# Attention rows of three slots in four chains, in place of four slots in three chains

## The chip, the cores and the metric

The kernel runs on one core of one Trainium2 chip. The metric is the device time of one execution in microseconds (us), lower is better. An engine is named as the profile names it: PE (TensorE), DVE (VectorE), ACT (ScalarE), POOL (GpSimd), SP (SyncE, which only issues DMAs here).

## The reference

A graph network on 6250 nodes and 100000 edges (`src`, `dst`, sorted by `dst`), 256 features. First three layers of max-pooling over incoming edges with two layer norms, then one layer of sparse attention with 8 heads whose rows are the sources and whose columns are the destinations of the edges:

```python
h = jnp.maximum(_layernorm(x), 0.0)
x = x + L0(h, src, dst)            # pool-max over edges, matmul, relu, layer norm: three times
h = jnp.maximum(_layernorm(x), 0.0)
q = (h @ Wq + bq).reshape(n, 32, 8) * 32 ** -0.5
k, v = (h @ Wk + bk).reshape(n, 32, 8), (h @ Wv + bv).reshape(n, 32, 8)
s = einsum('edh,edh->eh', q[src], k[dst])
m = segment_max(s, src); e = exp(s - m[src]); z = segment_sum(e, src)
out = segment_sum((e / z[src])[:, None, :] * v[dst], src)
x = x + out.reshape(n, -1) @ Wo + bo
```

## The kernel before

**Stages.** A projection; then three times a pass over the edges (`max_pass`, 87 batches of nine gathers, each gather 128 rows of 1 KB) and a pass over the nodes (`combine`, the last one `combine_project`, 49 tiles); then the attention pass, the carry over the ends of its chains (`carry_attention`), and a last pass over the nodes (`finish`). Each stage is a block with its own instruction list for every engine; `staged` writes those lists out so that stages of several batches interleave.

**Rows and slots.** For the attention the edges are sorted by source on the chip (during passes 1 and 2) and laid out in rows. A row belongs to one source node and holds up to `SLOT` = 4 of its edges; a node with more edges has several rows, one after the other; empty slots are masked by `empty`. Each of the 128 partitions holds `RP` = 234 rows, cut into `R` = 3 chains of `NBA` = 78 rows. In batch n every partition works on row n of each of its chains, so a batch has R x SLOT = 12 slots of 128 edges. A row hands its running maximum, sums and weighted values (`state`, 272 numbers) on to the next row of its chain if both are of the same node (`row_reset`, `row_fresh`). Where a node goes over the end of a chain, `carry_attention` joins the parts by scans over all 128 x R = 384 chain ends.

**A batch of the attention pass.** POOL issues one indirect gather for each slot (L1871): 128 rows of 2 KB, key and value, into `kv`, six batches of buffers deep. DVE multiplies the keys by the row's query (L1903, `multiply`, which waits for all twelve gathers of its batch), weighs the values of the batch before (L1909, `weigh`), sums the products by head (L1913), scales what the chain brings in (L1928, `hold`), masks (L1934), copies the next batch's new queries over the old ones (L1892, `renew`, `copy_predicated` with the mask `row_fresh`), finds the maximum (L1940) and adds up the state (L1945, L1956, L1950, L1960). ACT takes one exponential (L1985). PE adds the weighed values over the slots by identity matmuls (L1977). SP stores the state (L2000) and loads the queries of a later batch (L1995).

**What prepares it.** In pass 1 `Degrees` counts edges by node and finds the rows of each node (`own_rows`, L1019 to L1023: add SLOT - 1, shift right by 2) as small DVE instructions between the folds of the max. `RowNodes` (L1338 to L1352, beside the first `combine`) finds the node of each row: comparisons on DVE and two matmuls a tile into `total`, 234 columns. `Marks` makes the resets of the rows at the start of pass 3. `Spread`, beside pass 3, moves the 936 edges of a partition to their slots: 16 steps of `aim`, then 40 of `move`, two steps a batch. `Clear` zeroes the query table `qtab` in pass 2, one 384 KB store a batch. The query table is filled by scatters in `combine_project`.

**Memory.** The eight PSUM banks are three tensors, `trio`, `wide` and `tail`. The attention pass keeps the queries in `wide`, the sums over slots in `tail` and `trio`.

Of the kernel before, what the change touches and what calls it, by code (L numbers as in the profile page):

```python
# [19 lines left out]
F32, BF16, I32, I16 = mybir.dt.float32, mybir.dt.bfloat16, mybir.dt.int32, mybir.dt.int16  # L20
ALU, ACT, AX = mybir.AluOpType, mybir.ActivationFunctionType, mybir.AxisListType

P = 128
D = 256
# [6 lines left out]
ACC = D + HEADS  # L31
KV = 2 * D
STATE = ACC + HEADS
SLOT = 4
R = 3
UN = 7
J = 9
C = 3
STEPS = J // C
UB = 3  # L40
W = 1024
COLS = W.bit_length() - 1
LEVELS = COLS + P.bit_length() - 1
# [59 lines left out]
def gnn_kernel(nc, x, src, dst, wp1, bp1, wm1, bm1, wm2, bm2, wm3, bm3, g2, b2, g3, b3,  # L103
# [14 lines left out]
    RP = NBA * R  # L118
    SL = RP * SLOT
    NOROW = P * RP  # L120
    assert 0 < TAIL < P and 0 < LASTE < CH and PAD >= N and NBA % UB == 0


# [20 lines left out]
    with ExitStack() as top:  # L144
# [33 lines left out]
        nmr = sb(top, "nmr", [P, NT])  # L178
        rows_upto = sb(top, "rows_upto", [P, NT])
        rows_own = sb(top, "rows_own", [P, NT])  # L180
        trio = top.enter_context(nc.psum_tensor("trio", [P, 3 * 512], F32))
        wide = top.enter_context(nc.psum_tensor("wide", [P, 3 * 512], F32))
        tail = top.enter_context(nc.psum_tensor("tail", [P, 2 * 512], F32))
        bank = [t[:, n * 512:(n + 1) * 512] for t in (trio, wide) for n in range(3)] + [tail[:, n * 512:(n + 1) * 512] for n in range(2)]
        bank = bank[0:3] + [bank[6]] + bank[3:6] + [bank[7]]

# [702 lines left out]
        class Degrees:  # L889
# [116 lines left out]
            def own_rows(self, v):  # L1006
                v.wait_ge(s_pe.sem, s_pe.base + 1)
                for n, to in enumerate((self.by_dst, self.by_src)):
                    for half in range(2):
                        rows_of = slice(half * self.LOW, (half + 1) * self.LOW)  # L1010
                        cols = slice(n * self.HIGH + half, (n + 1) * self.HIGH, 2)
                        if half == n:
                            chain.inc(v.tensor_copy(to[rows_of, :], self.f_sums[rows_of, cols]))
                            yield
                        else:
                            chain.inc(v.tensor_scalar(to[rows_of, :], self.sums[rows_of, cols], -1.0, None, ALU.mult))
                            yield
                v.wait_ge(chain.sem, chain.base)
                chain.link(v.tensor_scalar(self.f_ti, self.by_src, SLOT - 1.0, None, ALU.add))  # L1019
                yield  # L1020
                chain.link(v.tensor_scalar(self.f_ti, self.f_ti, SLOT.bit_length() - 1, None, ALU.logical_shift_right))
                yield
                chain.link(v.tensor_copy(rows_own[:, :], self.f_ti))  # L1023
                v.sem_inc(s_dve.sem, 1)
                yield

# [130 lines left out]
        class Spread:  # L1157
# [53 lines left out]
            def vector(self, v):  # L1211
                def find(i, b):
                    if i * UB + b == self.FIND:
                        v.wait_ge(self.looked, 16 * R)
                        v.wait_ge(chain.sem, self.need)
                        v.tensor_tensor(self.at[:, :], self.first[:, 0, 0:1], self.own[:, :], ALU.add).then_inc(self.found, 1)
                        chain.inc(v.tensor_copy(chain_ix[:, :], self.first[:, :, 1]))
                        chain.link(v.scalar_tensor_tensor(out=row_fresh, in0=self.node, scalar=float(N), in1=self.fresh, op0=ALU.is_lt, op1=ALU.mult))

                def slot(at):  # L1220
                    def stage(i, b):
                        q = 2 * (i * UB + b - self.BEGIN) + at
                        if q < 0:
                            return
                        if q < 16:
                            self.aim(v, q)
                        elif q < 16 + 4 * COLS:
                            self.move(v, (q - 16) % 4, COLS - 1 - (q - 16) // 4)
                        elif q < 18 + 4 * COLS:
                            self.put(v, q - 16 - 4 * COLS)  # L1230
                    return stage
                return {1: [(0, find)], 2: [(0, slot(0))], 5: [(0, slot(1))]}

            def aim(self, v, q):
                a, b, ti, window = (x[:, :] for x in (self.a, self.b, self.ti, self.window))
                c = self.c
                one = ones[:, 0:1].to_broadcast([P, SL])
                if q == 0:
                    v.wait_ge(self.taken, 16)
                v.wait_ge(chain.sem, self.need)  # L1240
                if q == 0:
                    ins = v.tensor_scalar(ti, window, NODES.bit_length() - 1, None, ALU.logical_shift_right)
                elif q == 1:
                    ins = v.tensor_copy(a, ti)
                elif q == 2:
                    ins = v.tensor_tensor(b[:, 1:SL], a[:, 1:SL], a[:, 0:SL - 1], ALU.not_equal)
                elif q == 3:
                    ins = v.tensor_tensor(b, b, self.iota, ALU.mult)
                elif q == 4:
                    ins = v.tensor_tensor_scan(c, one, b, 0.0, ALU.mult, ALU.max)  # L1250
                elif q == 5:
                    ins = v.tensor_tensor(ti, self.iota, c, ALU.subtract)
                elif q == 6:
                    ins = v.tensor_scalar(ti, ti, SLOT - 1, None, ALU.bitwise_and)
                elif q == 7:
                    ins = v.tensor_copy(a, ti)
                elif q == 8:
                    ins = v.tensor_scalar(b, a, 0.0, None, ALU.is_equal)
                elif q == 9:
                    ins = v.tensor_tensor_scan(c, one, b, 0.0, ALU.mult, ALU.add)  # L1260
                elif q == 10:
                    ins = v.scalar_tensor_tensor(out=c, in0=c, scalar=float(SLOT), in1=a, op0=ALU.mult, op1=ALU.add)
                elif q == 11:
                    ins = v.tensor_scalar(ti, window, NODES - 1, None, ALU.bitwise_and)
                elif q == 12:
                    ins = v.tensor_scalar(a, ti, 1.0, None, ALU.add)
                elif q == 13:
                    ins = v.scalar_tensor_tensor(out=b, in0=c, scalar=-float(SLOT), in1=self.iota, op0=ALU.add, op1=ALU.subtract)
                elif q == 14:
                    ins = v.scalar_tensor_tensor(out=b, in0=b, scalar=float(NODES), in1=a, op0=ALU.mult, op1=ALU.add)  # L1270
                elif q == 15:
                    ins = v.scalar_tensor_tensor(out=self.value, in0=c, scalar=float(SL + SLOT), in1=b, op0=ALU.is_lt, op1=ALU.mult)
                self.need = chain.inc(ins)

# [31 lines left out]
        class RowNodes:  # L1306

            def __init__(self, space):  # L1310
                parts, start = [], 0
                for size in (RP, RP, UN * P, UN * P, UN * RP, 2 * RP):
                    parts.append(space[:, start:start + size])
                    start += size
                self.iota, self.all1, eq, gt, ge, ti = parts
                self.eq, self.gt, self.ge = (x.rearrange("p (u e) -> p u e", u=UN) for x in (eq, gt, ge))
                self.ti = ti.bitcast(I32)
                self.made, self.mm = Count(sem("node_made"), 0), Count(sem("node_mm"), 0)
                self.total = bank[7][:, 0:RP]
                self.const0 = const_base[0]  # L1320
                const_base[0] += 1
# [512 lines left out]
        def attention_pass(st, state, empty):  # L1834
            KB, QB = 6, 4
            kvs = [sb(st, f"kv{b}", [P, SLOT * R, KV]) for b in range(KB)]
            rooms = [weights[:, b * R * D:(b + 1) * R * D] for b in range(QB - 1)] + [pass_lists[:, b * R * D:(b + 1) * R * D] for b in range(2)]
            *qs, begun = (room.rearrange("p (r f) -> p r f", f=D) for room in rooms)
            held = sb(st, "held", [P, R, ACC])
            s = sb(st, "s", [P, SLOT + 1, R, HEADS])  # L1840
            row_max = sb(st, "row_max", [P, R, HEADS])
            w = shifted.rearrange("p (b e r h) -> p b e r h", b=UB, r=R, h=HEADS)
# [171 lines left out]
        def carry_attention(state):  # L2014
# [3 lines left out]
            with ExitStack() as st, block() as blk:  # L2018
# [8 lines left out]
                add = sb(st, "add", [P, R, ACC])  # L2027
                turned = [bank[k][:, 0:ALL] for k in range(4)]
                made, blocked = sb(st, "made", [P, ALL]), sb(st, "blocked", [P, ALL])
                carried = wide.rearrange("p (r x) -> p r x", r=R)  # L2030
                m0 = s_misc.base

                def chains_of(ap):
# [191 lines left out]
        w_q, w_kv = mat(w_q), mat(w_kv)  # L2225
        w_o, v_o, empty, shifted = parts_of(FREED, KC * D, D, SL, UB * (SLOT + 1) * R * HEADS)
        w_o = mat(w_o)
        assert max(KC * D + KC * KV + D + KV, 3 * R * D) <= FREED

        def find_empty(v):  # L2230
            chain.link(v.tensor_scalar(empty[:, :], dst_ix[:, 0:SL], 0.0, NEG, ALU.is_lt, ALU.mult))
# [2 lines left out]
        with scope() as l0:  # L2234
# [23 lines left out]
            with scope() as g:  # L2258
# [5 lines left out]
                    marks = Marks(c, dst_ix, CH, reset, fix_ix, flag, degrees.hot[:, :].bitcast(F32), C)  # L2264
                    max_pass(G, degrees, LayerInput(c, w_m1a, v_m1, True), marks)
                blocked = sb(g, "blocked", [P, P * C])
                combine(G, U, w_m1b, None, None, True, Carry(G, blocked, 1), RowNodes(G[1][:, :, :].rearrange("p k f -> p (k f)").bitcast(BF16)))
                with scope() as c:
                    clear = Clear(c)
                    max_pass(G, Sorting(sort, clear), LayerInput(c, w_m2a, v_m2, False), ahead=clear)  # L2270
# [42 lines left out]
```

## Time and profile before

| | |
|---|---|
| time, median of 3 runs (lowest to highest) | 4856.15 us (4855.05 to 4858.15) |
| the profiled execution: its own time, its span | 4848.88 us, 4847.1 us |
| busy share of the span: POOL, DVE, PE, ACT | 71%, 65%, 35%, 23% |
| attention gathers on POOL (L1871) | 936 times, 987 ns |
| max-pass gathers on POOL (L541) | 2349 times, 949 ns |

The span is that of one execution, from its first to its last instruction. A group of instructions is shown as line, engine, operation, output<-inputs, shapes, count, then busy time in all, mean ns of one, and the engine's idle time before them with what ended most of it. DMA-issuing instructions of SP are not counted as busy; the gathers on POOL are. In a timeline a row is start, duration, engine, line, operation, and in square brackets the engine's idle time before it and what ended it.

### The profile page before, as it was taken

How to read it: one execution, taken by the hardware profiler on the slowest of the kernel's cores; microseconds unless marked ns; L12 is line 12 of the kernel's file. 1: busy time of each engine (PE TensorE's matmuls, PEld its weight loads, DVE VectorE, ACT ScalarE, POOL GpSimd, SP SyncE). 2: the span in 40 equal slices, each digit the busy share in tenths (PEclk: the TensorE clock that was granted, in tenths of full speed). 3: DMA queues.
4: the chain of work that ended last, by engine and by line, in shares of the span. 5: the costliest groups of instructions: out<-in, count | busy, mean ns of one | idle time of the engine just before them, and what ended most of it. 6: DMA issues, size and time to landing. Idle time of an engine off the chain costs nothing. (4 is left out here: it accounts for less than half of the span.)

```text
span 4847.1 us, 27940 instructions
## 1 busy us (share of the span) xinstructions
PE 1710.1 (35%) x5261; PEld 1035.5 (21%) x5261; DVE 3135.9 (65%) x6298; ACT 1096.5 (23%) x2585; POOL 3461.3 (71%) x3612
## 2 busy tenths in 40 slices
PE   5434322106233312025222200019644454445546
PEld 4222211005111100014111100006322222222224
DVE  7888887645444444437455533338488888888886
ACT  5333322223222222224222222225200000000001
POOL 4777777766777777766777777765377777777764
PEclk8555555558555555557555555559867777777778
DMA  5666666656777777756666766655478887887875
GB/s 193 217 209 210 211 210 209 212 181 209 255 257 255 259 248 242 242 189 209 223 212 221 233 212 209 211 185 192 143 239 256 253 254 255 257 255 255 253 227 178
DMA packets 451437, 1083.65 MB, mean 224 GB/s; under 512 B 82637, under 2 KB 178524, under 8 KB 451263
## 3 DMA queue, kind: packets, MB, share of 16 engines
q0 software_dynamic: 203376, 598.29, 42.7%
q1 hardware_dynamic: 247886, 483.58, 26.9%
q14 instruction: 131, 1.07, 0.1%
q8 instruction: 44, 0.72, 0.1%
HBM read 656.78 MB, written 425.20 MB: 223 GB/s over the span
## 5 line engine op out<-in xcount | busy, mean ns | idle before, releaser
L541 POOL DMA_INDIRECT G<-tab,pass_lists x2349 | 2228.3, 949 | 725.0 <-issue 714.8
L561 DVE SCALAR_TENSOR_TENSOR G<-tail,pass_lists,G 128x256 f32<-128x256 f32 x1566 | 699.1, 479 | 1304.5 <-DMA G<-tab,pass_lists 1296.3
L1871 POOL DMA_INDIRECT kv<-kvtab,dst_ix x936 | 923.5, 987 | 285.1 <-issue 285.1
L602 ACT ACTIVATE tail<-G 128x512 f32<-128x512 f32 x783 | 471.0, 602 | 1768.1 <-DVE G L561 1726.3
L678 PE MATMUL tail<-weights,hT 128*128 128x256 f32 x588 | 304.9, 674 | 551.7 <-ACT hT L655 551.7
L1977 PE MATMUL tail<-kv,ident 128*128 128x512 f32 (+1 forms) x624 | 301.7, 653 | 360.9 <-DVE kv L1909 360.9
L1977 PE MATMUL trio<-kv,ident 128*128 128x512 f32 (+1 forms) x624 | 294.4, 640 | 295.4 <-DVE kv L1909 295.4
L604 ACT ACTIVATE wide<-G 128x256 f32<-128x256 f32 x783 | 296.8, 379 | 382.4 <-DVE G L561 371.1
L561 DVE SCALAR_TENSOR_TENSOR G<-wide,pass_lists,G 128x256 f32<-128x256 f32 x783 | 372.5, 476 | 0.8
L1903 DVE TENSOR_TENSOR kv<-kv,wide 128x3072 f32<-128x3072 f32 x78 | 261.7, 3355 | 167.9 <-DMA kv<-kvtab,dst_ix 167.9
L672 PE MATMUL tail<-ident,h 128*128 128x128 f32 x294 | 95.1, 426 | 625.5 <-DVE U L641 582.3
L678 PEld LDWEIGHTS tail<-weights,hT 128*128 128x128 f32 x588 | 172.6, 324 | 634.6 <-ACT hT L655 608.1
L1985 ACT ACTIVATE wide<-weights 128x120 f32<-128x120 f32 x78 | 21.4, 274 | 1205.9 <-DVE weights L1960 1205.9
L1977 PEld LDWEIGHTS tail<-kv,ident 128*128 128x128 f32 x624 | 157.6, 260 | 505.4 <-DVE kv L1909 377.0
L1909 DVE TENSOR_TENSOR kv<-kv,wide 128x3072 f32<-128x3072 f32 x78 | 261.1, 3347 | 0.3 <-ACT wide L1985 0.3
L1913 DVE TENSOR_REDUCE s<-kv 128x96 f32<-128x3072 f32 x78 | 261.0, 3346 | 0.0
L1379 PE MATMUL trio<-ident,G 128*128 128x128 f32 x18 | 4.5, 424 | 697.0 <-PEq L526 697.0
L1977 PEld LDWEIGHTS trio<-kv,ident 128*128 128x128 f32 x624 | 154.4, 255 | 435.4 <-DVE kv L1909 311.1
L1104 PE MATMUL trio<-hot 128*128 128x196 bf16 x783 | 142.2, 369 | 195.7 <-DVE hot L955 195.7
L672 PEld LDWEIGHTS tail<-ident,h 128*128 128x128 f32 x294 | 42.0, 201 | 734.3 <-issue 689.7
L955 DVE TENSOR_TENSOR hot<-wide,key_high 128x2156 bf16<-128x2156 f32 x72 | 170.4, 2367 | 0.0
L1104 PEld LDWEIGHTS trio<-hot 128*128 128x128 bf16 x783 | 114.1, 148 | 218.7 <-DVE hot L955 207.7
(340 smaller groups left out, 3281.4 us busy)
## 6 DMA issues: line engine op xcount, KB each, us to landing
hist<-G SPq DMA_DIRECT2D x783, 384.0 KB, 3.0
G<-tab,pass_lists POOLq DMA_INDIRECT x2349, 3.2
ahist<-state SPq DMA_DIRECT2D x78, 408.0 KB, 3.4
qtab<-zeros SPq DMA_DIRECT2D x78, 384.0 KB, 4.3
weights<-qtab SPq DMA_DIRECT2D x59, 384.0 KB, 5.7
tab<-o SPq DMA_DIRECT2D x147, 128.0 KB
kv<-kvtab,dst_ix POOLq DMA_INDIRECT x936, 3.9
h<-tab SPq DMA_DIRECT2D x98, 128.0 KB, 3.9
```

The source lines that it names most:

```text
L541: g.indirect_dma_start(G[b][:, k, :], None, tab, bass.IndirectOffsetOnAxis(src_ix[:, at:at + 1], 0)).then_inc(s_in[r].sem, 16)
L561: ins = v.scalar_tensor_tensor(out=G[b][:, k, :], in0=state2 if c == 2 else state[:, c, :], scalar=reset[:, at:at + 1], in1=G[b][:, k, :], ...
L602: a.activation(state, of[:, 0:2, :], ACT.Copy).then_inc(c_state.sem, 1)
L604: a.activation(state2, of[:, 2, :], ACT.Copy).then_inc(c_state.sem, 1)
L678: m = pe.matmul(self.product, self.hT[:, k * P:(k + 1) * P], self.w[:, k, :], start=(k == 0), stop=(k == KC - 1))
L955: v.tensor_tensor(to[n % self.RING][:, 0:some, :, :].rearrange("p k l e -> p (k l) e"), self.iota[:, None, 0:width].to_broadcast([P, 2 * s ...
L1104: m = pe.matmul(self.sums, self.low[n % self.RING][:, k, :, :], self.high[n % self.RING][:, k, :, :], start=(n == 0 and k == 0), stop=(n = ...
L1871: g.indirect_dma_start(kvs[n % KB][:, k, :], None, kvtab, bass.IndirectOffsetOnAxis(dst_ix[:, at:at + 1], 0)).then_inc(s_kv[n % KB], 16)
L1903: v.tensor_tensor(keys, keys, query[:, None, :, :].to_broadcast([P, SLOT, R, D]), ALU.mult).then_inc(c_scored, 1)
L1909: v.tensor_tensor(vals, vals, by_slot[:, :, None, :].to_broadcast([P, GATHERS, HD, HEADS]), ALU.mult).then_inc(c_weighed, 1)
L1913: keep("sums", i * UB + b, v.tensor_reduce(scores().rearrange("p e r h -> p (e r) h"), kvs[(i * UB + b) % KB][:, :, 0:D].rearrange("p k (h ...
L1977: m = pe.matmul(sums[n % 2][:, rs, :], ident[:, :], kvs[n % KB][:, e * R + rs.start:e * R + rs.stop, D:KV], start=(e == 0), stop=(e == SLO ...
```

## The change

`SLOT` becomes 3 and `R` becomes 4. With 6250 nodes and 100000 edges that makes 300 rows a partition in four chains of 75, 900 slots, and 75 batches of twelve gathers; states and queries of a batch have four rows in place of three (stores of 544 and loads of 512 KB in place of 408 and 384). Division by 4, a shift or a mask, becomes division by 3: in `own_rows` by the helper `divide` (ten steps), in `aim` by a multiplication by 683 and a shift by 11. Row numbers now go over 256, so `RowNodes` counts in float32, in place of bfloat16. The carry needs four banks for its 128 x 4 chain ends, so PSUM becomes one tensor of which the old ones are parts. Some buffers of the attention pass move.

```diff
-SLOT = 4
-R = 3
+SLOT = 3
+R = 4
...
+SHIFT = 11
+THIRD = -(-(1 << SHIFT) // SLOT)
...
-        trio = top.enter_context(nc.psum_tensor("trio", [P, 3 * 512], F32))
-        wide = top.enter_context(nc.psum_tensor("wide", [P, 3 * 512], F32))
-        tail = top.enter_context(nc.psum_tensor("tail", [P, 2 * 512], F32))
+        psum = top.enter_context(nc.psum_tensor("psum", [P, 8 * 512], F32))
+        trio, wide, tail = psum[:, 0:3 * 512], psum[:, 3 * 512:6 * 512], psum[:, 6 * 512:8 * 512]
...
-                chain.link(v.tensor_scalar(self.f_ti, self.by_src, SLOT - 1.0, None, ALU.add))
+                chain.link(v.tensor_scalar(self.f_has, self.by_src, SLOT - 1.0, None, ALU.add))
                 yield
-                chain.link(v.tensor_scalar(self.f_ti, self.f_ti, SLOT.bit_length() - 1, None, ALU.logical_shift_right))
-                yield
-                chain.link(v.tensor_copy(rows_own[:, :], self.f_ti))
+                yield from divide(v, self.f_has, SLOT, rows_own[:, :], self.f_stepped[0], self.f_ti, self.f_stepped[1])
...
                 elif q == 5:
-                    ins = v.tensor_tensor(ti, self.iota, c, ALU.subtract)
+                    ins = v.tensor_tensor(a, self.iota, c, ALU.subtract)
                 elif q == 6:
-                    ins = v.tensor_scalar(ti, ti, SLOT - 1, None, ALU.bitwise_and)
+                    ins = v.tensor_scalar(ti, a, float(THIRD), None, ALU.mult)
                 elif q == 7:
-                    ins = v.tensor_copy(a, ti)
+                    ins = v.tensor_scalar(ti, ti, SHIFT, None, ALU.logical_shift_right)
                 elif q == 8:
+                    ins = v.tensor_copy(b, ti)
+                elif q == 9:
+                    ins = v.scalar_tensor_tensor(out=a, in0=b, scalar=-float(SLOT), in1=a, op0=ALU.mult, op1=ALU.add)
...
-                for size in (RP, RP, UN * P, UN * P, UN * RP, 2 * RP):
+                for size in (RP, UN * P, UN * P, UN * RP):
                     parts.append(space[:, start:start + size])
                     start += size
-                self.iota, self.all1, eq, gt, ge, ti = parts
+                self.iota = counted
+                self.all1, eq, gt, ge = parts
...
-                self.ti = ti.bitcast(I32)
+                self.ti = counted.bitcast(I32)
...
-            rooms = [weights[:, b * R * D:(b + 1) * R * D] for b in range(QB - 1)] + [pass_lists[:, b * R * D:(b + 1) * R * D] for b in range(2)]
-            *qs, begun = (room.rearrange("p (r f) -> p r f", f=D) for room in rooms)
+            rooms = [weights[:, b * R * D:(b + 1) * R * D] for b in range(QB - 2)] + [pass_lists[:, 0:R * D]]
+            qs = [room.rearrange("p (r f) -> p r f", f=D) for room in rooms] + [sb(st, "q", [P, R, D])]
             held = sb(st, "held", [P, R, ACC])
+            begun = held[:, :, 0:D]
...
-                carried = wide.rearrange("p (r x) -> p r x", r=R)
+                carried = psum[:, 3 * 512:7 * 512].rearrange("p (r x) -> p r x", r=R)
```

Nothing else is rewritten; all loops and tiles over `R`, `SLOT`, `RP`, `SL` and `NBA` take the new sizes.

## Rows read from the trace of the kernel before

**Rows 1.** The page, part 1: busy time, share of the span and instructions of each engine.

```profile
PE 1710.1 (35%) x5261; PEld 1035.5 (21%) x5261; DVE 3135.9 (65%) x6298; ACT 1096.5 (23%) x2585; POOL 3461.3 (71%) x3612
```

**Rows 2.** The page, part 5: the gathers on POOL.

```profile
L541 POOL DMA_INDIRECT G<-tab,pass_lists x2349 | 2228.3, 949 | 725.0 <-issue 714.8
...
L1871 POOL DMA_INDIRECT kv<-kvtab,dst_ix x936 | 923.5, 987 | 285.1 <-issue 285.1
```

**Rows 3.** Busy time by stretch: mid attention pass, carry, first combine.

```profile
3640.00:4540.00 900.00, 445.43 (x926) 233.30 (x927) 786.83 (x754) 15.90 (x58) 688.32 (x696) 0.72 0.81 255
4735.90:4768.80 32.90, 6.93 (x26) 5.39 (x26) 13.31 (x23) 1.08 (x2) 6.04 (x6) 0.60 0.14 43
1077.00:1152.00 75.00, 65.80 (x392) 54.30 (x392) 46.36 (x197) 33.66 (x97) 50.43 (x52) 0.91 0.57 174
```

**Rows 4.** Waits from 3650 to 4800 us: total, times, longest.

```profile
DVE kv L1903 <- DMA kv<-kvtab,dst_ix: 134.4, 69, 2.5
```

**Rows 5.** Timeline: first and last of the 78 multiplies of the attention pass.

```profile
3517.89 3.35 DVE L1903 TENSOR_TENSOR kv<-kv,wide 128x3072 f32<-128x3072 f32 x1 [12.61 <-DMA kv<-kvtab,dst_ix]
...
4711.21 3.35 DVE L1903 TENSOR_TENSOR kv<-kv,wide 128x3072 f32<-128x3072 f32 x1 [1.98 <-DMA kv<-kvtab,dst_ix]
```

**Rows 6.** Timeline of two batches of the attention pass, POOL and DVE, cut.

```profile
4008.11 0.94 POOL L1871 DMA_INDIRECT kv<-kvtab,dst_ix  x1 [0.30 <-issue]
...
4009.36 1.03 POOL L1871 DMA_INDIRECT kv<-kvtab,dst_ix  x1 [0.30 <-issue]
4009.49 0.96 DVE L1892 COPY_PREDICATED wide<-row_node,weights 128x768 f32<-128x768 int32 x1
...
4010.70 0.94 POOL L1871 DMA_INDIRECT kv<-kvtab,dst_ix  x1 [0.30 <-issue]
...
4013.20 3.35 DVE L1903 TENSOR_TENSOR kv<-kv,wide 128x3072 f32<-128x3072 f32 x1 [1.24 <-DMA kv<-kvtab,dst_ix]
...
4023.19 0.95 POOL L1871 DMA_INDIRECT kv<-kvtab,dst_ix  x1 [0.30 <-issue]
...
4024.32 0.96 DVE L1892 COPY_PREDICATED wide<-row_node,weights 128x768 f32<-128x768 int32 x1
4024.44 1.64 POOL L1871 DMA_INDIRECT kv<-kvtab,dst_ix  x1 [0.30 <-issue]
...
4028.66 3.35 DVE L1903 TENSOR_TENSOR kv<-kv,wide 128x3072 f32<-128x3072 f32 x1 [1.90 <-DMA kv<-kvtab,dst_ix]
```

**Rows 7.** Timeline: a copy and the gather begun under it, early and late.

```profile
3559.35 0.96 DVE L1892 COPY_PREDICATED wide<-row_node,pass_lists 128x768 f32<-128x768 int32 x1
3559.44 1.68 POOL L1871 DMA_INDIRECT kv<-kvtab,dst_ix  x1 [0.30 <-issue]
...
4706.78 0.96 DVE L1892 COPY_PREDICATED wide<-row_node,weights 128x768 f32<-128x768 int32 x1
...
4706.89 1.66 POOL L1871 DMA_INDIRECT kv<-kvtab,dst_ix  x1 [0.30 <-issue]
```

**Rows 8.** Groups by shape: three DVE instructions of the attention pass.

```profile
L1903 DVE TENSOR_TENSOR kv<-kv,wide 128x3072 f32<-128x3072 f32 x78 | 261.7, 3355 | 167.9 <-DMA kv<-kvtab,dst_ix 167.9
...
L1928 DVE TENSOR_TENSOR held<-state,wide 128x792 f32<-128x792 f32 x78 | 75.6, 970 | 0.0
L1892 DVE COPY_PREDICATED wide<-row_node,weights 128x768 f32<-128x768 int32 x59 | 56.7, 961 | 0.0
```

**Rows 9.** DMA queues from 3700 to 4600 us: packets, MB, engine share.

```profile
q0 software_dynamic: 55659, 182.41, 66.6%
q1 hardware_dynamic: 16704, 47.05, 14.0%
```

**Rows 10.** Timeline of the first combine, one tile, cut.

```profile
1107.25 0.26 PE L1345 MATMUL tail<-G 128*128 128x234 bf16 x1
...
1107.35 0.26 PE L1346 MATMUL tail<-G 128*128 128x234 bf16 x1
...
1107.45 0.43 DVE L1530 TENSOR_TENSOR G<-wide,U 128x256 f32<-128x256 f32 x1 [0.34 <-PE wide L1602]
```

More of the change, by code:

```diff
@@ L120, in gnn_kernel @@
     NOROW = P * RP
+    assert all((n * THIRD) >> SHIFT == n // SLOT for n in range(SL))
     assert 0 < TAIL < P and 0 < LASTE < CH and PAD >= N and NBA % UB == 0
@@ L1224, in stage @@
                             return
-                        if q < 16:
+                        if q < 18:
                             self.aim(v, q)
-                        elif q < 16 + 4 * COLS:
-                            self.move(v, (q - 16) % 4, COLS - 1 - (q - 16) // 4)
                         elif q < 18 + 4 * COLS:
-                            self.put(v, q - 16 - 4 * COLS)
+                            self.move(v, (q - 18) % 4, COLS - 1 - (q - 18) // 4)
+                        elif q < 20 + 4 * COLS:
+                            self.put(v, q - 18 - 4 * COLS)
                     return stage
@@ L1251, in aim @@
                 elif q == 5:
-                    ins = v.tensor_tensor(ti, self.iota, c, ALU.subtract)
+                    ins = v.tensor_tensor(a, self.iota, c, ALU.subtract)
                 elif q == 6:
-                    ins = v.tensor_scalar(ti, ti, SLOT - 1, None, ALU.bitwise_and)
+                    ins = v.tensor_scalar(ti, a, float(THIRD), None, ALU.mult)
                 elif q == 7:
-                    ins = v.tensor_copy(a, ti)
+                    ins = v.tensor_scalar(ti, ti, SHIFT, None, ALU.logical_shift_right)
                 elif q == 8:
+                    ins = v.tensor_copy(b, ti)
+                elif q == 9:
+                    ins = v.scalar_tensor_tensor(out=a, in0=b, scalar=-float(SLOT), in1=a, op0=ALU.mult, op1=ALU.add)
+                elif q == 10:
                     ins = v.tensor_scalar(b, a, 0.0, None, ALU.is_equal)
-                elif q == 9:
+                elif q == 11:
                     ins = v.tensor_tensor_scan(c, one, b, 0.0, ALU.mult, ALU.add)
-                elif q == 10:
+                elif q == 12:
                     ins = v.scalar_tensor_tensor(out=c, in0=c, scalar=float(SLOT), in1=a, op0=ALU.mult, op1=ALU.add)
-                elif q == 11:
+                elif q == 13:
                     ins = v.tensor_scalar(ti, window, NODES - 1, None, ALU.bitwise_and)
-                elif q == 12:
+                elif q == 14:
                     ins = v.tensor_scalar(a, ti, 1.0, None, ALU.add)
-                elif q == 13:
+                elif q == 15:
                     ins = v.scalar_tensor_tensor(out=b, in0=c, scalar=-float(SLOT), in1=self.iota, op0=ALU.add, op1=ALU.subtract)
-                elif q == 14:
+                elif q == 16:
                     ins = v.scalar_tensor_tensor(out=b, in0=b, scalar=float(NODES), in1=a, op0=ALU.mult, op1=ALU.add)
-                elif q == 15:
+                elif q == 17:
                     ins = v.scalar_tensor_tensor(out=self.value, in0=c, scalar=float(SL + SLOT), in1=b, op0=ALU.is_lt, op1=ALU.mult)
@@ L1306, in gnn_kernel, with __init__ @@
         class RowNodes:
-            def __init__(self, space):
+            def __init__(self, space, counted):
                 parts, start = [], 0
-                for size in (RP, RP, UN * P, UN * P, UN * RP, 2 * RP):
+                for size in (RP, UN * P, UN * P, UN * RP):
                     parts.append(space[:, start:start + size])
                     start += size
-                self.iota, self.all1, eq, gt, ge, ti = parts
+                self.iota = counted
+                self.all1, eq, gt, ge = parts
                 self.eq, self.gt, self.ge = (x.rearrange("p (u e) -> p u e", u=UN) for x in (eq, gt, ge))
-                self.ti = ti.bitcast(I32)
+                self.ti = counted.bitcast(I32)
                 self.made, self.mm = Count(sem("node_made"), 0), Count(sem("node_mm"), 0)
@@ L2227, in gnn_kernel @@
         w_o = mat(w_o)
-        assert max(KC * D + KC * KV + D + KV, 3 * R * D) <= FREED
+        assert max(KC * D + KC * KV + D + KV, 2 * R * D) <= FREED
         def find_empty(v):
@@ L2266, in gnn_kernel @@
                 blocked = sb(g, "blocked", [P, P * C])
-                combine(G, U, w_m1b, None, None, True, Carry(G, blocked, 1), RowNodes(G[1][:, :, :].rearrange("p k f -> p (k f)").bitcast(BF16)))
+                combine(G, U, w_m1b, None, None, True, Carry(G, blocked, 1), RowNodes(G[1][:, :, :].rearrange("p k f -> p (k f)").bitcast(BF16), G[0][:, :, :].rearrange("p k f -> p (k f)")[:, J * D - RP:]))
                 with scope() as c:
```

## Prediction

> **What bounds the kernel now.** I read the page first, then busy time by stretch, then, for the attention pass alone, its waits, its timeline and its DMA queues. Over the whole span no engine is full; GpSimd (POOL) is busiest, at 71% [rows 1]. The instruction groups say why: 2349 gathers of the three max passes at 949 ns and 936 of the attention pass at 987 ns, each with about 0.30 us of "issue" before it, so nothing else is being waited for between them [rows 2]. The change is aimed at the 936. In that pass a batch is 12 gathers, one batch of DVE work, one load and one store. In the middle of the pass DVE is busy 87% and POOL 76% [rows 3], but POOL's share leaves out its 0.30 us a gather. What ends last is told by the wait: DVE's first instruction of a batch waits for its gathered rows, 69 times in that stretch and never over 2.5 us [rows 4]. So the pass runs at POOL's pace, DVE close behind. First to last multiply is 1193.3 us for 77 steps: 15.50 us a batch [rows 5].
>
> Ten gather steps take 12.49 us (4010.70 to 4023.19), 1.249 each, so twelve free ones are 14.99 us; the other 0.5 us is one slow gather a batch. The timeline shows which. The gather at 4024.44 takes 1.64 us in place of 0.95. It starts 0.12 us after COPY_PREDICATED (L1892, the new query rows, on DVE), which ends at 4025.28, and the gather ends 0.80 after that. One batch earlier the gather starts 0.13 us before the copy and takes 1.03 [rows 6]. First and last such pair of the pass again end 0.81 apart; in 74 batches, those caught all end 0.80 to 0.82 after the copy, those begun before it (seven) are nearly free [rows 7]. So a gather begun under the copy waits for its end: stall = length of the copy - start offset - 0.14.
>
> The Trainium skill (SBUF — State Buffer, Who interferes with whom) has the reason: a DVE instruction with two SBUF inputs takes the port that GpSimd reads through, and the later of the two blocks to its end. The copy reads mask and rows from SBUF, so the rule fits the 0.80. By it alone each batch's stall would lengthen with the copy, and the sum would be -12 us (the second rival); by the offsets of the rows it is -58.
>
> **The change, part by part.**
> *Gathers.* 78 batches of 12 become 75 of 12: 936 to 900. Each stays 128 rows of 2 KB. Worth 3 batches, if a batch costs the same.
>
> *DVE per batch.* The big three keep 3072 elements (12 slots either way). What goes by rows grows by a third: L1928 792 to 1056 elements, L1892 and L1950 768 to 1024. L1903's 3355 ns for 3072 elements against L1892's 961 for 768 make 1.04 ns an element [rows 8], so +0.28, +0.27 and +0.27 us; I put 0.03 for the short instructions. DVE now needs 87.4% of 15.50 us a batch, 13.55; it becomes 14.40. That is under the 14.99 of twelve free gathers, so DVE does not become the bound, but its slack falls from 1.95 to about 0.6.
>
> *TensorE.* 8 identity matmuls of 512 or 256 columns become 6 of 512, the same 3072 columns; PE is half idle there [rows 3]. Nothing.
>
> *DMA.* Software queue 66.6% and hardware queue 14.0% of 15.5 us are 10.3 and 2.2 us of engine time a batch [rows 9]. The load and store grow by a third, +0.72 us: 13.2 us, 87% of a 15.1 us batch. It still fits; if it did not, 14.99 is the floor anyway.
>
> *The stall.* This decides. I follow where the first gather after a batch's last one starts, relative to the copy. If the gather is caught, that last gather's rows come late too: the next multiply starts 3.38 us after the copy's end (4025.28 to 4028.66). If it is free, the multiply starts 5.09 us after the last gather's start (4008.11 to 4013.20); other free batches have 4.9 to 5.0. Multiply to copy is 11.12 us. Now, after a caught batch (offset and stall make 0.96 - 0.14 = 0.82 together, whatever the offset), the next offset is 14.99 + 0.82 - 0.96 - 3.38 - 11.12 = +0.35 (less where rows land later, 0.26 on average): caught again. After a free one it is 14.99 + 1.25 - 5.0 - 11.12 = +0.12: caught again as well. So the old batch always falls back under the copy. After the change the copy is 1.23 long and 11.40 after the multiply. After a caught batch: 14.99 + 1.09 - 1.23 - 3.38 - 11.40 = +0.07, or -0.02 with the later landing: a toss-up. After a free one: 14.99 + 1.25 - 5.0 - 11.40 = -0.16: the gather starts before the copy and is free, and so is the next. Free batches keep themselves free; the second gather starts at +1.09, when the copy has 0.14 us left, which costs nothing. With landing times scattering by 0.1 us, a run of free batches seldom ends and a run of caught ones ends soon. I take one batch in ten caught at 1.05 us and 0.05 us for the rest of the copy or later landings: 15.15 us. Lower bound: no stall, 14.99. Upper bound: always caught just behind the copy's start, 14.99 + 1.07 = 16.06.
>
> 74 steps of 15.15 are 1121.1 against 1193.3: **-72.2 us** (-84 to -5).
>
> *Before and behind the pass.* One more begun gather ahead of the first kv gather, 1.25 (L1871's step). The tail behind the last multiply repeats L1928, L1950 for two more batches, +0.8. The carry works on 512 columns in place of 384: in its stretch of 32.9 us DVE is busy 13.3, PE 6.9, ACT 1.1 [rows 3], nearly all in a chain; a third of that is 7.1, less what PE overlaps and fixed parts, 6.3; the four scatters in place of three add 1.3. Its gathers are covered by the scans. Together +7.6 (6 to 9).
>
> *combine, first layer.* The count of L1345/L1346 multiplies 128x234, now 128x300, two a tile. PE runs without gaps there (65.8 of 75 us busy) [rows 3], a 128x234 bf16 matmul starts 0.10 us after the other, a 128x300 one would take 0.028 more, so +0.055 a tile, 49 tiles: +2.7. The comparison (L1338) reads float32 in place of bf16. If it goes at the 1.04 ns an element of rows 8, I estimate +0.25 a tile, and DVE sits idle 0.34 us before each tile's sum [rows 10]: hidden; without that cover it would be 12 us. Bounds +1 to +12.
>
> *The passes.* Pass 3 gets one more before_row gather on POOL, the bound: +1.25. The eight more steps of the row division are small DVE fillers in pass 1, where POOL's gathers at 0.95 + 0.30 us set the pace [rows 2]: hidden, 2 us if not. Two more steps in Spread, but each of some 60 on 900 in place of 936 elements: hidden, and as SBUF-to-SBUF work it may hold up a gather or two, ±1. Marks over 300 columns delay DVE 1 us while POOL fills 27 tiles: hidden. The clearing stores of pass 2 are 512 KB in place of 384, 75 in place of 78; a gather there still costs POOL its 1.25 us, and I expect POOL to stay the bound. 0 to +3. I put 0.5 for all of these.
>
> Sum: -72.2 + 1.25 + 0.8 + 7.6 + 2.7 + 1.25 + 0.5 = **-58 us**. The profiled run took 4848.88 with a span of 4847.1, and becomes 4791; the median of the three timed runs is 7.3 higher, 4856.15, and becomes **4798**.
>
> **Rivals.** A change under 0.2%, 9.7 us, is what this measurement can't tell from none.
> 1. *The stall stays 0.5 us.* Batches cost 15.50: 74 x 15.50 is -46.4, with +14.1 elsewhere -32: 4824. For it: the mean has been steady for 74 batches. Against it: the offsets above, which move by 0.28.
> 2. *The stall grows by the copy's 0.27* (15.77): -26.3 + 14.1 = -12: 4844. Same evidence against it.
> 3. *Locked behind the copy's start, the other side.* Every batch is caught at +0.0 to +0.1, and the larger load and store delay the last rows. From 16.07 us a batch the kernel is slower by over 0.2%: 74 x 16.07 = 1189.2, -4.1 + 14.1 = +10: 4866. For it: the +0.07 above. Against it: below 0.02 the gather slips free, and a later landing pushes it there.
> 4. *The passes don't hide their parts* (combine's DVE becomes its bound, +9; DMA in pass 2, +3): 4810. Adds to any of them.
>
> **Chances and range.** Slipping free 0.50 (4798, its own range 4785 to 4812, from 14.99 and from 15.3 us a batch); rival 1 0.22; rival 2 0.13; rival 3 0.10, half of it at 16.0 and thus within 0.2%; the rest 0.05, spread. Leaving out the lowest and what lies above rival 2, the range is 4785 to 4852. Faster: 0.50 + 0.22 + most of rival 2 and of the rest, 0.83. Same 0.10. Slower 0.07.
>
> **What the profile after would show.** L1871: 900 times, mean near 955 ns in place of 987; if it is 987, rival 1, 1010 rival 2, 1030 or more rival 3. Multiply to multiply 15.1 us; L1892 1.23 us at 11.40 behind the multiply; the first gather 0.1 to 0.3 us ahead of it. Carry near 40 us. I am wrong if L1892 costs something else than by element (the offset turns on 0.1 us), if more DMA work makes the last rows land later by several tenths, or if other two-input instructions on DVE catch the second gather.

## The result, and the profile after

| | before | after |
|---|---|---|
| time, median of 22 runs (lowest to highest) | 4853.6 us (4848.25 to 4858.36) | 4846.31 us (4823.35 to 4852.61) |
| ratio after/before, 95% interval | | 0.9981 (0.9974 to 0.9987) |
| profiled execution: its own time, its span | 4848.88 us, 4847.1 us | 4838.44 us, 4836.5 us |

Faster by 7 us, within the 0.2% that was called no change; the forecast was 58 us. The time lies in the range, the gain does not come near the one forecast. The time after also scatters over 29 us from run to run, the time before over 10.

The page after, part 5: the gathers of the max passes and of the attention pass, and its first multiply (answer to [rows 2, 8]).

```profile
L543 POOL DMA_INDIRECT G<-tab,pass_lists x2349 | 2225.5, 947 | 726.4 <-issue 714.6
...
L1877 POOL DMA_INDIRECT kv<-kvtab,dst_ix x900 | 917.4, 1019 | 274.2 <-issue 270.8
...
L1909 DVE TENSOR_TENSOR kv<-kv,psum 128x3072 f32<-128x3072 f32 x75 | 251.6, 3354 | 134.2 <-DMA kv<-kvtab,dst_ix 134.2
```

36 gathers are gone, but one takes 1019 ns on average in place of 987. Against the 946 of gathers that nothing holds up (experiment 1), 12 x (1019 - 946) is 0.88 us of stall a batch, where 0.5 was. The max passes have not moved.

The timeline after: first and last multiply (answer to [rows 5]).

```profile
3520.95 3.35 DVE L1909 TENSOR_TENSOR kv<-kv,psum 128x3072 f32<-128x3072 f32 x1 [12.38 <-DMA kv<-kvtab,dst_ix]
...
4696.30 3.35 DVE L1909 TENSOR_TENSOR kv<-kv,psum 128x3072 f32<-128x3072 f32 x1 [1.46 <-DMA kv<-kvtab,dst_ix]
```

1175.35 us for 74 steps, 15.88 a batch in place of 15.50: the pass gains 18.0 us, not 72. The first multiply is 3.1 us later, and from the last multiply to the end of the span it is 140.2 us in place of 135.9. -18.0 + 3.1 + 4.3 is -10.6, the difference of the two spans.

The timeline after, a batch in the middle, POOL and DVE, cut (answer to [rows 6]).

```profile
4012.42 3.35 DVE L1909 TENSOR_TENSOR kv<-kv,psum 128x3072 f32<-128x3072 f32 x1 [1.68 <-DMA kv<-kvtab,dst_ix]
...
4023.82 1.22 DVE L1898 COPY_PREDICATED psum<-row_node,weights 128x1024 f32<-128x1024 int32 x1
4023.88 1.98 POOL L1877 DMA_INDIRECT kv<-kvtab,dst_ix  x1 [0.30 <-issue]
4026.16 0.94 POOL L1877 DMA_INDIRECT kv<-kvtab,dst_ix  x1 [0.30 <-issue]
...
4028.30 3.35 DVE L1909 TENSOR_TENSOR kv<-kv,psum 128x3072 f32<-128x3072 f32 x1 [1.53 <-DMA kv<-kvtab,dst_ix]
```

The lines show a loop. The copy starts 11.40 us after the multiply at 4012.42 and takes 1.22. A gather begun 0.06 us behind the copy's start (its *offset*) takes 1.98 us, and the next multiply starts 3.26 us after the copy's end; that last stretch, up to the arrival of the rows, is called the *landing* below. From the fourth step (multiply to multiply) on all 71 look like this, at offsets of 0.02 to 0.34 us, 0.17 on average. The length of a batch is then 11.39 + 1.22 + 3.30, 15.9 us. It is rival 3, locked just behind the copy's start.

Counting the gathers from the end of the pass shows one thing that the prediction had wrong: the caught gather is not the first one after a batch's last, it is the last one itself, the twelfth of the batch that the next multiply waits for. In the kernel before it is so too. That is why its rows "come late too", and why the loop closes. The sums of the prediction are not changed by it: they count from the copy either way.

### The profile page after: what moved, and what is told of

Read it like the earlier page. It is cut to its first block and busy times, and to the rows that moved or that the text cites. A ratio compares the mean times of both kernels' runs of the same rounds, so it can differ in the third digit from the quotient of the medians.

```text
span 4836.5 us, 27181 instructions
## 1 busy us (share of the span) xinstructions
PE 1685.6 (35%) x4921; PEld 953.9 (20%) x4921; DVE 3165.4 (65%) x6269; ACT 1096.0 (23%) x2582; POOL 3457.2 (71%) x3580
## 5 line engine op out<-in xcount | busy, mean ns | idle before, releaser
L563 DVE SCALAR_TENSOR_TENSOR G<-psum,pass_lists,G 128x256 f32<-128x256 f32 x2349 | 1036.1, 478 | 1302.8 <-DMA G<-tab,pass_lists 1296.0
L1877 POOL DMA_INDIRECT kv<-kvtab,dst_ix x900 | 917.4, 1019 | 274.2 <-issue 270.8
L604 ACT ACTIVATE psum<-G 128x512 f32<-128x512 f32 x783 | 471.0, 601 | 1765.8 <-DVE G L563 1723.2
L1983 PE MATMUL psum<-kv,ident 128*128 128x512 f32 x900 | 571.7, 801 | 663.4 <-DVE kv L1915 663.4
L680 PE MATMUL psum<-weights,hT 128*128 128x256 f32 x588 | 304.9, 673 | 553.0 <-ACT hT L657 553.0
L1983 PEld LDWEIGHTS psum<-kv,ident 128*128 128x128 f32 x900 | 228.4, 264 | 1006.6 <-DVE kv L1915 725.5
L606 ACT ACTIVATE psum<-G 128x256 f32<-128x256 f32 x783 | 296.7, 379 | 383.4 <-DVE G L563 372.4
L1909 DVE TENSOR_TENSOR kv<-kv,psum 128x3072 f32<-128x3072 f32 x75 | 251.6, 3354 | 134.2 <-DMA kv<-kvtab,dst_ix 134.2
L680 PEld LDWEIGHTS psum<-weights,hT 128*128 128x128 f32 x588 | 172.4, 324 | 636.3 <-ACT hT L657 609.8
L1915 DVE TENSOR_TENSOR kv<-kv,psum 128x3072 f32<-128x3072 f32 x75 | 251.0, 3346 | 0.3 <-ACT psum L1991 0.3
L1104 PE MATMUL psum<-hot 128*128 128x196 bf16 x783 | 142.2, 370 | 195.6 <-DVE hot L957 195.6
L957 DVE TENSOR_TENSOR hot<-psum,key_high 128x2156 bf16<-128x2156 f32 x72 | 170.3, 2366 | 0.0
L1809 PE MATMUL psum<-weights,full 128*128 128x256 f32 (+1 forms) x392 | 138.0, 495 | 13.5 <-DVE G L1734 13.3
```

The source lines that it names most:

```text
L563: ins = v.scalar_tensor_tensor(out=G[b][:, k, :], in0=state2 if c == 2 else state[:, c, :], scalar=reset[:, at:at + 1], in1=G[b][:, k, :], ...
L604: a.activation(state, of[:, 0:2, :], ACT.Copy).then_inc(c_state.sem, 1)
L606: a.activation(state2, of[:, 2, :], ACT.Copy).then_inc(c_state.sem, 1)
L680: m = pe.matmul(self.product, self.hT[:, k * P:(k + 1) * P], self.w[:, k, :], start=(k == 0), stop=(k == KC - 1))
L957: v.tensor_tensor(to[n % self.RING][:, 0:some, :, :].rearrange("p k l e -> p (k l) e"), self.iota[:, None, 0:width].to_broadcast([P, 2 * s ...
L1104: m = pe.matmul(self.sums, self.low[n % self.RING][:, k, :, :], self.high[n % self.RING][:, k, :, :], start=(n == 0 and k == 0), stop=(n = ...
```

## The experiments

All ratios are to the kernel before on the same chip (4845.69 us for the second runs of 1, 2 and 4; 4843.73 for max_first_before in 2 and for z_first, the kernel of 3). "Us a batch" is first to last multiply in the profile. Three of the chips were unlike the others, and are told of in 5.

**1. Take away the port, leave the copy.** The mask goes to a free PSUM bank, so the copy keeps place and length but has one SBUF input.

```diff
-            fresh_of = row_fresh.bitcast(I32).rearrange("p (r n) -> p r n", r=R)
+            mask = bank[2][:, 0:RP].bitcast(I32)
+            fresh_of = mask.rearrange("p (r n) -> p r n", r=R)
...
+                    chain.link(v.tensor_copy(mask, row_fresh.bitcast(I32)))
                     chain.link(v.tensor_copy(query, begun[:, :, :]))
```

> The changed kernel with the mask of the query copy held in PSUM, so that the copy has one SBUF input; its place and length stay. Theory (the copy holds up the last gather of the next batch because it reads two SBUF inputs, and that gather's rows start the next batch): no gather is caught, all stay at 0.95 us, a batch costs 14.99 us in place of 15.88, about 4780 us in all. Rival (any instruction of this length on DVE, or DMA load, holds up the gather): batches stay at 15.9 us, 4846 us. Rival (DMA or DVE is the real bound near 15.9): gathers may be short but multiply to multiply stays at 15.9 us.

The same edit on the kernel before:

> The same single edit on the kernel before. Theory: 77 steps fall from 15.50 to 14.99 us, about 4814 us. Together with the run on the changed kernel this gives what three slots in four chains are worth without the stall: 3 batches of 14.99, less about 7 us outside the pass, 38 us. Rival (stall has another cause): 4854 us.

Both were run twice, and the second pair on a chip like the first of all:

> Again the changed kernel with the mask in PSUM: the first run fell on a chip that gives the kernel before 5463 us and shows waits of several us that the first profiles don't have; there no gather begun under the copy was held up. On a chip like the first: no gather held up, 15.0 us a batch, about 66 us less than the changed kernel (4780 us). Rival (the real bound lies near 15.9 us): no change in time, 4846 us.

> Again the kernel before with the mask in PSUM. Theory: 15.0 us a batch in place of 15.5, 39 us less, about 4814 us, ratio 0.992. Rival: no change.

Measured in the second pair: changed kernel 0.986 (0.9844 to 0.9877), 4777.76 us, 15.02 us a batch, L1878 947 ns; kernel before 0.9926 (0.9909 to 0.9942), 4808.76 us, 15.01 us a batch, L1872 946 ns. The timeline of the kernel before with this edit, the copy and the gather begun under it:

```profile
3675.62 0.96 DVE L1893 COPY_PREDICATED wide<-trio,pass_lists 128x768 f32<-128x768 int32 x1
3675.71 0.95 POOL L1872 DMA_INDIRECT kv<-kvtab,dst_ix  x1 [0.30 <-issue]
```

Begun 0.09 us behind the copy's start, it takes 0.95 us; with the mask in SBUF a gather at the same offset took 1.68 [rows 7]. The copy's length has not changed. So it is the second SBUF input that held the gathers up, all of the stall was this, and without it both kernels run at the pace of twelve free gathers, 14.99. The rule of the Trainium skill that the prediction cites is borne out for a gather that comes second: it waits for the copy's end. For a copy that comes second it is not: a copy begun under a running gather took 0.96 or 1.23 us as ever, and at most 1.00 or 1.27 when the two began within 0.02 us of each other. The rivals, another bound near 15.9 or the load on the DMA engines, are out: with more bytes in flight a batch takes 15.02.

The pair also gives what three slots in four chains are worth without the stall: 0.986 against 0.9926, 31 us, where 38 were expected. First to last multiply goes from 1155.7 us (77 steps) to 1111.2 (74), 44.5 less, as expected; some 13.5 us of it go elsewhere (15 by the two profiled spans), and not 7.

**2. Move the copy by 0.3 us.** The maximum goes ahead of it.

```diff
-                                        (0, pass_on), (0, maximum), (2, put_z), (0, top), (2, put), (0, differ)])
+                                        (0, maximum), (0, pass_on), (2, put_z), (0, top), (2, put), (0, differ)])
```

> The changed kernel with the row maximum ahead of the query copy in place of behind it: the copy starts 0.22 us later after the multiply. Theory (the batch is locked just behind the start of the copy, at an offset of about +0.15): the last gather now starts before the copy and is free, the one after it is caught for 0.1 to 0.2 us at most, a batch costs 15.1 to 15.2 us, about 4790 us. Rival (the loop copy, landing, multiply, copy is a closed chain in any order): 0.22 us more a batch, 4862 us. Rival (order on DVE doesn't matter): 4846 us.

> Again the changed kernel with the maximum ahead of the copy, which then starts at 11.6 to 11.7 us after the multiply in place of 11.39. Theory (locked just behind the copy's start): the last gather is free, 15.1 to 15.2 us a batch, about 4790 us. Rival (closed chain in any order): 0.2 to 0.3 us more a batch, 4862 us or more. Rival (order doesn't matter): 4846 us.

Measured in the second run: 0.989 (0.9874 to 0.9907), 4792.13 us, 15.22 us a batch, the copy 11.69 us after the multiply. Moving work ahead of the copy makes the batch 0.66 us shorter, which no closed chain would do. The 0.2 us over 15.02 are mostly the gather behind the last one: in most batches it begins 0.67 to 1.0 us behind the copy's start and is held for up to 0.42 us. Then the same on the kernel before:

> The kernel before with the maximum ahead of the copy, 11.41 us after the multiply, for a chip without the long waits: about 15.1 us a batch in place of 15.50, ratio 0.9935. Rival (closed chain): ratio 1.005.

0.993 (0.9913 to 0.9946), 4810.04 us, 15.03 us a batch, copy at 11.46. The kernel before stood in the same lock, at its own offset, and the same reorder opens it.

**3. Move it by 0.1 us.** Only the short sum of z goes ahead of the copy.

```diff
-                                        (0, pass_on), (0, maximum), (2, put_z), (0, top), (2, put), (0, differ)])
+                                        (2, put_z), (0, pass_on), (0, maximum), (0, top), (2, put), (0, differ)])
```

> The changed kernel with one short instruction ahead of the copy, for a chip without the long waits. Locked at +0.15 with the edge at +0.02: 15.1 to 15.4 us a batch, ratio 0.988 to 0.992. Rival (closed chain): 1.000. Rival (order doesn't matter): 0.998.

0.9909 (0.9893 to 0.9926), 4801.8 us, copy at 11.50, 15.39 us a batch on average. The average hides two states. The timeline shows both, first at 3720 us, then at 4016:

```profile
3719.96 1.23 DVE L1898 COPY_PREDICATED psum<-row_node,weights 128x1024 f32<-128x1024 int32 x1
3720.00 2.00 POOL L1877 DMA_INDIRECT kv<-kvtab,dst_ix  x1 [0.30 <-issue]
...
4016.07 0.98 POOL L1877 DMA_INDIRECT kv<-kvtab,dst_ix  x1 [0.30 <-issue]
4016.25 1.22 DVE L1898 COPY_PREDICATED psum<-row_node,weights 128x1024 f32<-128x1024 int32 x1
```

Begun 0.04 us behind the start of the copy, the last gather takes 2.00 us, and such a batch 16.0; begun 0.18 ahead of it, 0.98, and 15.1. A third of the batches are caught, up to ten in a row; the longest run of free ones is 27, the others up to five. This is the pattern that the prediction forecast for the changed kernel itself, where it put the caught ones at a tenth.

**4. Move it to mid batch.** The copy goes behind the weighing, 6.54 us after the multiply.

```diff
                     def renew(n):
+                        if n:
+                            v.wait_ge(c_scored, n)
...
-                    staged(v, NBA, UB, [(0, multiply), (1, weigh), (0, add_up), (0, before), (2, hold), (0, block_empty),
-                                        (0, pass_on), (0, maximum), (2, put_z), (0, top), (2, put), (0, differ)])
+                    staged(v, NBA, UB, [(0, multiply), (1, weigh), (0, pass_on), (0, add_up), (0, before), (2, hold), (0, block_empty), (0, maximum), (2, put_z), (0, top), (2, put), (0, differ)])
```

> The changed kernel with the query copy moved up behind the weighing, 6.5 us after the multiply in place of 11.4 (with a wait that the multiply has read the queries). Theory: the copy then falls on a gather in the middle of a batch, whose rows no one waits for yet; the ninth gather after the one that released the multiply starts 1.02 us after the copy's start and is held for 0.07 us at most. No feedback through the multiply; 15.0 to 15.1 us a batch, about 4785 us. Rival (a stall of a fixed size wherever the copy stands): 15.9 us, 4846 us. Rival (a gather in mid batch is caught at random, 0.48 us on average): 15.5 us, 4816 us.

> Again the changed kernel with the copy behind the weighing, 6.53 us after the multiply. Theory: it holds up no gather that the next multiply waits for; the offset of the ninth gather is 1.02, its stall 0.07; 15.0 to 15.1 us a batch, about 4785 us. Rival (a fixed stall wherever the copy stands): 4846 us. Rival (caught at random, 0.48 us on average): 15.5 us a batch, 4816 us.

Measured in the second run: 0.9881 (0.9864 to 0.9897), 4789.18 us, 15.18 us a batch. The timeline:

```profile
3667.18 1.23 DVE L1900 COPY_PREDICATED psum<-row_node,pass_lists 128x1024 f32<-128x1024 int32 x1
3668.02 1.20 POOL L1877 DMA_INDIRECT kv<-kvtab,dst_ix  x1 [0.30 <-issue]
```

The same copy, still with two SBUF inputs, costs this gather 0.25 us (offset 0.84) in place of 0.9, since nothing that the next multiply waits for is under it and the offset is not fed back. Over the pass it costs 0.17 us a batch, about what 15.18 is over the 15.02 of experiment 1. That is more than the 0.07 forecast, as the offset came out at 0.72 to 1.08, 0.92 on average, in place of 1.02.

**5. The runs on other chips.** The first runs of the kernels of 1 (mask_after, mask_before), 2 (max_first) and 4 (copy_weigh), and two runs each of z_first, max_first_before and copy_last (the copy as the last instruction of the batch) fell on chips where every kernel takes over 5400 us, the kernel before 5439 to 5466. What was expected of copy_last:

> The changed kernel with the copy as the last instruction of the batch, about 13.2 us after the multiply. The last gather is long through; the second one after it starts about 0.7 us behind the start of the copy and is held for 0.3 to 0.4 us, and no landing waits for it: 15.3 us a batch, ratio about 0.990. Rival (the stall is the length of the copy wherever it stands): 15.9 us, 0.998. Rival (the next multiply now waits for the copy, which becomes a chain with the query load): slower.

| kernel | ratio there (95% interval) |
|---|---|
| mask_after, mask_before | 0.9937 (0.992 to 0.9954), 0.9991 (0.9974 to 1.0008) |
| max_first, copy_weigh | 0.9947 (0.993 to 0.9963), 0.9954 (0.9938 to 0.9971) |
| z_first, twice | 0.9954 (0.9933 to 0.9974), 0.9948 (0.9929 to 0.9966) |
| max_first_before, twice | 1.0019 (1.0005 to 1.0034), 0.9989 (0.997 to 1.0008) |
| copy_last, twice | 0.9983 (0.9962 to 1.0003), 0.9972 (0.9956 to 0.9988) |

The waits of mask_after on such a chip, from 3900 to 5200 us:

```profile
DVE state L1957 <- remote: 196.4, 27, 18.6
POOL kv L1878 <- remote: 132.5, 25, 12.4
```

DVE's sum L1957 waits there up to 18.6 us. In the kernel it waits for the semaphore that TensorE raises behind its sums over the slots. The profile names no releaser on this core ("remote"), and TensorE's own records end earlier: the last twelve matmuls ahead of one such wait run from 4215.99 to 4223.26, while L1957 waits until 4231.14. Mostly three batches of 14.25 us are followed by two of 17 to 24, and the pass no longer runs at POOL's pace: 17.2 us a batch whether gathers are held up (max_first) or not (mask_after). These runs say nothing on the lock, copy_last was never seen elsewhere and stays open, and what delays the semaphore on those chips is not known. Even so, mask_after shows the gather free: a gather begun 0.27 us behind the copy's start (4188.58 and 4188.31) takes 0.95.

## Why the prediction was wrong, point by point

**The step that failed** is "a toss-up" in *The stall*: the term of 15.15 us a batch was mis-sized, it measured 15.88. The sum was 14.99 + 1.09 - 1.23 - 3.38 - 11.40 = +0.07, or -0.02 with a landing of 3.47, with the edge at +0.02. Copy length, its place and the pitch of the gathers came out as forecast (1.22, 11.39, 1.25). The landing did not: 3.13 to 3.45 us after the copy's end, 3.30 on average, where the prediction took 3.38 or 3.47 from the trace of before. With 3.30 the next offset is +0.15 (measured 0.17 on average), and the gather is always caught. One to two tenths of a microsecond thus decided over 54 us (74 times 15.88 less 15.15).

The trace of before could have told this, for there the landing goes with the hold. At offsets under 0.1 us, held for over 0.7, the rows land 3.35 us after the copy's end on average, at 0.1 to 0.2 3.42, at 0.2 to 0.4 3.51, above 0.4, held for under 0.4, 3.79. One of the last kind:

```profile
3574.69 0.96 DVE L1892 COPY_PREDICATED wide<-row_node,weights 128x768 f32<-128x768 int32 x1
3575.17 1.29 POOL L1871 DMA_INDIRECT kv<-kvtab,dst_ix  x1 [0.30 <-issue]
...
3579.74 3.35 DVE L1903 TENSOR_TENSOR kv<-kv,wide 128x3072 f32<-128x3072 f32 x1 [2.61 <-DMA kv<-kvtab,dst_ix]
```

Held for 0.34 us, its rows land 4.09 us after the copy's end. After the change every hold is long (0.92 us on average, 0.74 at least), so the short landings are the ones to count with; among holds that long the landing no longer goes with the hold. Why the rows of a gather held up longer land sooner was not tried; that the queues have had more time to empty is only argued.

**The other half of the step**, free batches staying free, was too sure as well. The profile after has one free gather at -0.28, and the next is caught at +0.03, where -0.16 was forecast:

```profile
3562.77 0.94 POOL L1877 DMA_INDIRECT kv<-kvtab,dst_ix  x1 [0.30 <-issue]
3563.05 1.23 DVE L1898 COPY_PREDICATED psum<-row_node,q 128x1024 f32<-128x1024 int32 x1
3564.01 1.08 POOL L1877 DMA_INDIRECT kv<-kvtab,dst_ix  x1 [0.30 <-issue]
...
3577.85 1.23 DVE L1898 COPY_PREDICATED psum<-row_node,weights 128x1024 f32<-128x1024 int32 x1
3577.88 2.02 POOL L1877 DMA_INDIRECT kv<-kvtab,dst_ix  x1 [0.30 <-issue]
```

The prediction let the second gather start at +1.09 at no cost. Here it starts at +0.96 and is held for 0.13 us, and this pushes the next last gather back under the copy. With the copy 0.1 us later (experiment 3) free runs hold. So the mechanism was right, and the kernel stood on the wrong side of its edge.

**The chances** gave this case 0.10, at 16.07 us and 4866; it came at 15.88 and 4846. It called the sum a toss-up and then gave the two states 0.50 and 0.10. For a sum whose sign decides between two states and whose error is larger than its value, the two should have had like chances.

**The gathers, DVE, TensorE, DMA.** Right. L1898 takes 1224 ns, L1934 1243, L1956 1213 (1228, 1245 and 1215 forecast). The stretch from 3640 to 4540 us (answer to [rows 3]) has DVE at 90% and POOL at 77%, and a DMA share of 0.81, as before. DVE's own work is 14.3 us of a batch of 15.88, where 14.40 was forecast.

```profile
3640.00:4540.00 900.00, 429.88 (x681) 171.60 (x680) 810.50 (x740) 16.02 (x57) 693.27 (x679) 0.72 0.81 266
```

**Outside the pass**, 14.1 us were forecast and 7.4 measured in this pair of profiles, some 13.5 in the pair of experiment 1. The place of the first multiply alone varies by 3.6 us over five profiles of the changed kernel and its variants, and by 5.4 over three of the kernel before and its, though they differ ahead of it by one short copy at most. The carry, from its first memset (4723.53) to its first scatter (4751.13), is 27.6 us in place of 23.1, and one scatter more is 1.3: +5.8, forecast 7.6. The tail from the last multiply to that memset is 27.2 in place of 27.8, so the 0.8 for it was not there. The first combine is right: its tile costs 1.34 us (1107.95 to 1109.29, L1350) in place of 1.28 to 1.29.

```profile
1107.95 0.29 PE L1350 MATMUL psum<-G 128*128 128x300 bf16 x1
...
1109.29 0.29 PE L1350 MATMUL psum<-G 128*128 128x300 bf16 x1
```

**Where the gain went.** Three batches less at 15.50 are 46.5 us. A copy longer by 0.26 and later by 0.28, in a loop that it closes, less a landing sooner by 0.22 (3.30 in place of 3.52 over all caught ones), makes a caught batch 0.32 us longer, 15.91 in place of 15.59. Before, seven free batches of 14.7 stood among them, after it one, which adds 0.06. 0.38 on each of 74 batches is 28.5 us given back, what 46.5 leaves over the 18.0 measured. 7.4 go outside the pass. 46.5 - 28.5 - 7.4 is 10.6.

**The better version.** The change with its mask in PSUM (experiment 1) beats both kernels: 0.986 of the kernel before. No gather is held up in it, and gathers at 1.25 us set the pace; DVE's order was not moved on top of it, so that it no longer matters is not shown.

## What to carry to other kernels

When a busy engine looks like the bound with a few per cent to spare, look for the one slow instance in each period and for what it runs into; here a mean of 987 ns hid one gather in twelve at up to 1.73 us. A port conflict on the instruction that a loop waits for is paid again in the length of the loop, so give the long DVE instruction one input in PSUM, or put it under transfers that no one waits for yet. And where two states are a tenth of a microsecond apart, forecast both, and shift the order by one short instruction to see on which side the kernel stands.

## What the runs showed of the hardware

A gather that GpSimd begins 0.02 to 1.0 us after the start of a COPY_PREDICATED with mask and data in SBUF (and before its last 0.2 us) ends 0.80 to 0.82 us after the copy, in all of over 140 cases of the kernels before and after, with copies of 0.96 and 1.22 us; begun 0.1 to 0.3 us ahead of it, it takes 0.94 to 1.04. With the mask in PSUM a gather takes 0.94 to 1.04 us at any offset, and the copy takes as long as with it in SBUF. The hold goes one way: the copy got longer only where the gather began within 0.02 us of it, by 0.05 us at most. The lock gives a batch two lengths: experiment 3 shows batches of 15.1 and of 16.0 us in one execution. That the changed kernel's spread from 4823 to 4853 us comes from a varying number of free batches fits this, but only one of its 22 runs has a profile. And there are chips on which this kernel takes 12% longer, with waits between engines of up to 18.6 us, so that a ratio from one does not carry to the other: mask_after is at 0.986 here and at 0.9937 there.
